# Graph kernel: source one-hots of graph attention made during propagation, and fewer blocks at its last two stages

## What is computed

```python
# L0: ten steps of propagation, w = 1/sqrt(deg(src)*deg(dst)), sums over dst into src
for _ in range(10): out = segment_sum(out[col] * w, row) * 0.9 + h * 0.1
# L1: graph attention (one self loop per node added)
h = x @ W
e = leaky_relu((h @ att_src)[src] + (h @ att_dst)[dst], 0.2)
e = exp(e - segment_max(e, dst)[dst])
out = tanh(segment_sum(h[src] * e[:, None], dst) / segment_sum(e, dst) + bias)
# L2: dot attention, four heads, softmax over the edges of each source
q, k, v = x[rows] @ qW, x[cols] @ kW, x[cols] @ vW ; res = segment_sum(softmax(q.k) * v, rows)
# L3: mean aggregation
out = segment_sum(x[src] @ W + b, dst) / deg
```

## Time and profile before

| | us |
|---|---|
| median of three runs | 1568.0 (1566.27 to 1568.41) |
| the profiled execution | 1561.1 |
| its span, first to last instruction | 1559.3 |
| building counts and buckets | 0 to about 300 |
| propagation, ten turns | about 300 to 838 |
| graph attention: norm, masks and maxima | 840 to 974 |
| graph attention: slot loop | 974 to 1183 |
| dot attention: norm, projection | 1183 to 1223 |
| dot attention: slot loop | 1223 to 1459 |
| mean aggregation | 1464 to 1559 |

### The profile page before, as it was taken

The page is one execution under the profiler, slowest core; times in us unless marked ns, Lnnn a source line. Parts: engine busy times, 40 slices in busy tenths (PEclk is TensorE's granted clock), DMA queues, the critical chain, the costliest instruction groups (busy, mean ns, idle before and its releaser), DMA issues. The chain is left out here.

```text
span 1559.3 us, 45179 instructions
## 1 busy us (share of the span) xinstructions
PE 1244.0 (80%) x18543; PEld 1185.1 (76%) x18544; DVE 1234.2 (79%) x2306; ACT 583.3 (37%) x1271; POOL 355.8 (23%) x211
## 2 busy tenths in 40 slices
PE   4689888399999899998996400888883999999378
PEld 3278777399899899998995300888883899999378
DVE  6989888577677677676756899999996899999733
ACT  0057788200000000000000686566664677777311
POOL 1400000000000000000001010688882455555200
PEclk7868888699999999999998655999996999999689
DMA  0013334386678577676621474555534276775382
GB/s 11 0 61 115 121 114 141 104 334 266 225 272 287 208 277 275 219 262 251 245 73 54 154 261 161 213 213 213 213 130 193 89 270 263 279 283 221 141 332 90
DMA packets 88813, 297.54 MB, mean 191 GB/s; under 512 B 22399, under 2 KB 23976, under 8 KB 88604
## 3 DMA queue, kind: packets, MB, share of 16 engines
q1 hardware_dynamic: 66668, 231.86, 41.2%
q10 hardware_dynamic: 21600, 61.45, 10.3%
q0 software_dynamic: 336, 1.20, 0.3%
HBM read 188.31 MB, written 106.16 MB: 189 GB/s over the span
## 5 line engine op out<-in xcount | busy, mean ns | idle before, releaser
L1327 PE MATMUL psum<-work,count 128*128 128x192 f16 x6250 | 523.7, 248 | 35.7 <-issue 35.7
L1327 PEld LDWEIGHTS psum<-work,count 128*128 128x128 f16 x6250 | 521.6, 99 | 37.8 <-issue 36.9
L964 ACT ACTIVATE work<-work 128x1248 f32<-128x1248 f32 (+1 forms) x6 | 7.2, 1203 | 584.2 <-DVE work L947 584.1
L1672 PE MATMUL psum<-count 128*128 128x98 f16 x625 | 113.2, 209 | 114.6 <-DVE count L1726 99.2
L1718 POOL TENSOR_TENSOR count<-count 128x970 bf16<-128x970 f32 (+1 forms) x75 | 175.5, 2366 | 73.5 <-ACT count L1711 73.5
L1944 PE MATMUL psum<-count 128*128 128x100 f16 (+1 forms) x1875 | 176.6, 207 | 9.8 <-DVE count L2028 7.1
L1246 DVE SCALAR_TENSOR_TENSOR work<-psum,small,work 128x96 f32<-128x96 f32 x250 | 79.3, 317 | 123.7 <-PE psum L1327 123.4
L1945 PE MATMUL psum<-count 128*128 128x100 f16 (+1 forms) x1875 | 176.5, 207 | 0.1
L1944 PEld LDWEIGHTS psum<-count 128*128 128x128 f16 x1875 | 162.6, 98 | 14.8 <-DVE count L2028 11.1
L1945 PEld LDWEIGHTS psum<-count 128*128 128x128 f16 x1875 | 164.1, 98 | 0.2 <-issue 0.2
L2007 POOL TENSOR_TENSOR count<-count 128x1000 bf16<-128x1000 f32 (+1 forms) x75 | 133.1, 1775 | 108.2 <-ACT count L1993 108.2
(11 more groups left out here) (290 smaller groups left out, 2733.7 us busy)
## 6 DMA issues: line engine op xcount, KB each, us to landing
count<-onehots_by_src SPq DMA_DIRECT2D x75, 800.0 KB, 6.7
count<-bucket_rows_by_dst SPq DMA_DIRECT2D x50, 800.0 KB, 4.3
x<-bucket_rows_by_src SPq DMA_DIRECT2D x75, 400.0 KB, 5.8
onehots_by_src<-x ACTq DMA_DIRECT2D x75, 400.0 KB, 6.1
count_f<-count SPq DMA_DIRECT2D x25, 800.0 KB, 7.5
count<-count_turned SPq DMA_DIRECT2D x25, 800.0 KB, 5.6
count<-count_f SPq DMA_DIRECT2D x17, 800.0 KB, 4.2
count_turned<-x SPq DMA_DIRECT2D x25, 416.0 KB, 2.4
```

The lines of the kernel that those rows point to most:

```text
L1327: last = nc.tensor.matmul(bank[i % BANKS], count16[:, j, i * P:(i + 1) * P], y[par][:, j, :], start=(j == 0), stop=(j == TILES - 1))
L1672: nc.tensor.matmul(ps[:, at:at + GW], node_hot[SRC][t % 2][:, s, :], high[:, s, :], start=True, stop=False, skip_group_check=True)
```

## The change

What it does:

1. In propagation 50 more node halves are made and stored: graph attention's source one-hots, 128 x 1600 each, to a new tensor in HBM. There are now 150 node halves and 50 edge halves, three to one, placed behind the updates of tiles 0 to 22 of the first nine turns, 200 in 207 slots. Each is one load of 400 KB, one compare and one store of 400 KB. A tile of the counts is stored behind every sixth load.
2. In graph attention's slot loop the compare of the source nodes is gone (25 of 128 x 3200). SyncE loads the finished one-hots instead of the spread rows, 800 KB a tile as before, into four buffers instead of two; its wait is now for the tile's gathering by TensorE.
3. The work that makes the next round's one-hots moves from its own block into the main blocks of both slot loops, behind their last instructions and behind a branch.
4. Mean aggregation's second block is merged into its layer norm block; semaphores take the barrier's place. SyncE loads twelve tiles ahead without a stop.

The diff's core (the rest is the passing of arguments and the same thing for several rounds):

```diff
@@ propagate
-    pieces = Pieces(node_halves, steps_space.take(HALF_TILES[0][1] * P, F16), ...)
+    pieces = Pieces(node_halves, 0, 6 * TILES, steps_space.take(HALF_TILES[0][1] * P, F16), ...)
     LAST = K_STEPS - 1
-    assert LAST * 20 >= PIECES * 6 // 5
+    TURNS = 23
+    SLOTS = LAST * TURNS
...
-                        q = 20 * turn + i - 1
-                        if turn < LAST and 1 <= i <= 20 and q % 6 < 5:
-                            spots.compare(dve, pieces, 5 * (q // 6) + q % 6)
+                        q = TURNS * turn + i
+                        if turn < LAST and i < TURNS and (q + 1) * pieces.total // SLOTS > q * pieces.total // SLOTS:
+                            spots.compare(dve, pieces, q * pieces.total // SLOTS)
@@ Spots.row, Spots.one_hot: node halves from 4 * TILES on
+        return self.by_dst[bass.ds(k, 1), w - 2 * TILES, SRC].rearrange("k s n -> k (s n)")[:, half * HALF_ROW:(half + 1) * HALF_ROW]
+        hots = self.hot_by_src[:, w, :] if w < 2 * TILES else self.hot_by_dst[:, w - 2 * TILES, :]
@@ graph_attention
+    source_hot = [node_hot[SRC][0], *(v.rearrange("p (t n) -> p t n", n=P) for v in spread[SRC]), node_hot[SRC][1]]
+    SOURCES = len(source_hot)
...
+    def load_source_hot(sp, t):
+        sp.dma_start(source_hot[t % SOURCES].rearrange("p t n -> p (t n)"), hot_by_dst[:, t, :]).then_inc(S["source_hot_%d" % (t % SOURCES)], 16)
...
+                for t in range(2, SOURCES):
+                    load_source_hot(sp, t)
                 for t in range(2, TILES):
-                    for i, v in enumerate((SRC, DST)):
-                        sp.wait_ge(S["node_hot"], 2 * (t - 2) + i + 1)
-                        load_spread(sp, k, t, v)
+                    sp.wait_ge(S["node_hot"], t - 1)
+                    load_spread(sp, k, t)
+                    if t + 2 < TILES:
+                        sp.wait_ge(S["gathered"], (t - 1) * PER)
+                        load_source_hot(sp, t + 2)
...
                         if s0 == 0:
-                            pe.wait_ge(S["node_hot"], 2 * t + 2)
+                            pe.wait_ge(S["source_hot_%d" % (t % SOURCES)], 16 * (t // SOURCES + 1))
+                            pe.wait_ge(S["node_hot"], t + 1)
...
-                spot_nodes(SRC, 0)
-                spot_nodes(DST, 0)
+                spot_nodes(0)
                 spot_edges(0)
...
                             if s0 == 0:
-                                spot_nodes(SRC, t + 1)
+                                spot_nodes(t + 1)
                             elif s0 == GROUP:
-                                spot_nodes(DST, t + 1)
-                            else:
                                 spot_edges(t + 1)
@@ both slot loops, VectorE (SyncE and ScalarE alike)
                 add(TILES - 2)
-                add(TILES - 1)
+                def add_and_compare():
+                    add(TILES - 1)
+                    following.compare(dve)
+                if_one(dve, m, lambda: add(TILES - 1), add_and_compare)
-        spot_next_round(nc, m, pieces, k + 1, ids_dram, by_src, hot_by_src)
@@ mean_aggregate
-        if_one(sp, m, lambda: load_first(sp, 0, 2 * UNDER_WAY))
-        sp.wait_ge(weights_loaded, 32)
+        if_one(sp, m, lambda: one_loads(sp), lambda: count_loads(sp))
+        store(sp)
...
+                if s == 0:
+                    pe.wait_ge(parts_set, 2)
                 for j in range(TILES):
+                    for k, (t0, _) in enumerate(HALVES_OF_NODES):
+                        if s == 0 and j == t0:
+                            pe.wait_ge(low_made, k + 1)
...
     def one_loads(sp):
-        load_first(sp, 2 * UNDER_WAY, READY)
+        load_first(sp, 0, READY)
...
-    with nc.Block() as block:
-        @block.sync
+    layernorm_relu(nc, m["norm"], x, h, sq, ..., ready, sync=load_ahead, tensor=products, gpsimd=set_up, vector_before=dot_vector_end,
+                   vector_between=identity_and_inverse, vector_after=low_parts, scalar_after=scalar_end)
```

More of the change, by code:

```diff
@@ L968, in _, with __init__, load, compare @@
             scalar_after(act)
-def spot_next_round(nc, m, pieces, k, ids_dram, by_src, hot_by_src):
-    spots = m["spots"]
-    with nc.Block() as block:
-        @block.sync
[L976 to L996, removed]
+class NextRound:
+    def __init__(self, m, pieces, k, ids_dram):
+        self.m, self.pieces, self.k, self.ids_dram = m, pieces, k, ids_dram
+    def load(self, sp):
+        if self.pieces.edge is not None:
+            self.m["spots"].load_ids(sp, self.pieces, self.k, self.ids_dram)
+        for n in range(self.pieces.nodes):
+            self.m["spots"].load(sp, self.pieces, self.k, n)
+        self.m["spots"].wait_stored(sp, self.pieces)
+    def compare(self, dve):
+        dve.sem_inc(self.m["spots"].counted, 1)
+        for piece in range(self.pieces.total):
+            self.m["spots"].compare(dve, self.pieces, piece)
+        self.m["spots"].wait_stored(dve, self.pieces)
+    def store(self, act):
+        self.m["spots"].stores(act, self.pieces)
+        self.m["spots"].wait_stored(act, self.pieces)
 class Residual:
@@ L1140, in propagate, with is_edge, edge_of, node_of @@
+    def is_edge(self, piece):
+        return self.per > 0 and piece % self.per == 1
+    def edge_of(self, piece):
+        return piece // self.per
+    def node_of(self, piece):
+        if not self.per:
+            return piece
+        group, i = divmod(piece, self.per)
+        return group * (self.per - 1) + i - (i > 1)
+def propagate(nc, m, ins, cnt_dram, cnt16_dram, ids_dram, by_src, by_dst):
     W = TILES * D
@@ L1277, in _ @@
             spots.load_ids(sp, pieces, 0, ids_dram)
-            for n in range(NODE_HALVES):
-                spots.load(sp, pieces, 0, n, by_src)
+            for n in range(pieces.nodes):
+                spots.load(sp, pieces, 0, n)
                 store_count_tile(n)
@@ L1296, in _ @@
         def _(act):
-            spots.stores(act, pieces, hot_by_src)
+            spots.stores(act, pieces)
         @block.tensor
@@ L1360, in propagate, with _ @@
     with nc.Block() as block:
+        @block.gpsimd
+        def _(pool):
+            clear_semaphores(nc, spots.all())
         @block.vector
@@ L1652, in graph_attention @@
     with nc.Fori(0, rounds_of(nc, m)) as k:
+        following = NextRound(m, pieces, k + 1, ids_dram)
         with nc.Block() as block:
```

212 lines of the change are left out of this document (118 added, 94 removed).

## The result

| | before | after |
|---|---|---|
| median | 1567.1 us (1563.0 to 1568.4, 4 runs) | 1606.6 us (1604.8 to 1612.2, 4 runs) |
| ratio | | 1.0265 (95%: 1.0237 to 1.0293) |
| profiled execution, its span | 1561.1, 1559.3 | 1612.2, 1610.4 |

The changed kernel is 2.7% slower. The forecast was 1551, and 1606.6 lies above the whole range. I divide the 51.1 us first, stage by stage.

What follows compares the result with a forecast made beforehand. It took graph attention's slot loop as bound by what VectorE's compares and GpSimd share, and propagation by TensorE. Terms -17.5 + 10 - 4 - 6 = -17.5 us, from a median of 1568.0 to 1551 us, range 1534 to 1578.

Steps and rivals of the forecast that it cites:

- Parts 3 and 4: Next round's work moved behind dot attention, -4 us; mean aggregation in one block, first matmul earlier, -6 us.
- Part 1: Graph attention's slot loop without source compares: 7.91 us a tile falls to 7.2, -17.5 us, bounds -8 and -28.
- the turns: Graph attention's loop: VectorE's compares and GpSimd's subtractions exclude each other; each removed compare brings 0.85 us, 0.70 taken.
- rival (c): Graph attention's loop hardly gains, VectorE's time becoming waits for ScalarE or GpSimd: 7.8 us a tile, -3, 1565; chance 0.12.
- The floor: Graph attention's loop: the lower bound is TensorE's 6.8 us a tile, a gain of -28 us; as a rival, chance 0.15.
- Part 2: Propagation with 50 more compares, loads and stores: +10 us, bounds 0 and +40.
- the buffers' cycle: Propagation: load, compare, store and gaps take 12.6 us for four halves; 52.5 us a turn against 51.
- The bandwidth reckoning: Propagation: demand of 388 GB/s inside the 23 slots lies within the 318 to 413 seen in 2 us stretches.
- (a): Propagation becomes bound by its transfers, buffers' cycle longer than 13.5 us: +40 instead of +10, 1580 us; chance 0.16.

Runs made afterwards that it cites:

- e1_ends_only: The kernel before with only the next round's work moved into dot attention's slot loop and mean aggregation in one block: 1556.4 us, ratio 0.9937.
- g1_edges_third: The changed kernel with the old propagation, the edge compare of graph attention's loop in the third group of slots instead of the second: 1536.6 us, ratio 0.9812.
- three buffers: The kernel before with three buffers for node halves in place of four, no other work changed: 1573.0 us.
- counts late: The changed kernel with the count tiles' stores moved behind the last load, into propagation's tenth turn: 1592.9 us.
- all 25 slots: The changed kernel with its 200 pieces spread over all 25 tiles of a turn instead of tiles 0 to 22: 1601.8 us.
- five buffers: The changed kernel with a fifth node buffer in propagation, room made by leaving some one-hots and ids out: 1562.7 us.
- five, counts late: The changed kernel with a fifth node buffer and the count tiles stored in propagation's tenth turn: 1572.5 us.

## Why the prediction was wrong, step by step

**Parts 3 and 4 were right.** -4 and -6 were forecast; the rows give -4.0 and, to the first matmul, -6.1, of which 1.2 us is given back inside the stage. `e1_ends_only` gives 9.9 us for both.

**Part 1 was right on the turns and failed on the list of what moves.** The two engines do take turns, a removed compare is worth far less than its 2.04 us of busy time (19.0 us over 25 tiles are 0.76), and `g1_edges_third` shows the tile of 7.2 us and a loop 19.0 us shorter than before (208.0 - 189.0), where -17.5 was forecast. But the prediction never priced that the edge compare goes to the second group. There it begins during GpSimd's second subtraction, as at 1110.79, and ends 1.68 us behind it, with the weighing, the rounding and the next subtraction after it. That is the step that failed in the loop: -17.5 us was forecast and -0.4 came. So rival (c) came true in its size, for another reason than the one given: VectorE's time didn't move into the wait for ScalarE, it is one compare that stands in GpSimd's way. "Against it: VectorE has no idle time now" was no argument, since idle time appeared at once, 9 us in 50, and changed nothing. The floor was also taken wrongly: not TensorE's 6.8 us a tile but the ring of GpSimd and ScalarE, 7.35 us in the tile shown, which the third group's place already reaches (189.0 us for the loop against 189.5). So that the 7.2 us of the forecast were met in `g1_edges_third` is in part luck: the sum had taken one turn of 0.85 us from three, but there the edge compare's turn is off the chain too, and the ring stops the gain at the same figure.

The Trainium skill, SBUF — State Buffer, section "SBUF: two separate sides", which has the two engines exclude each other for whole instructions, is borne out by these rows: the same edge compare takes 1.81 us begun just as a subtraction ends, and 2.87 us begun 1.19 us before one's end (1110.79 against 1111.98). The rule should have been applied to the moved compare too.

**Part 2 failed in one step of the buffers' cycle.** Its sum was right: 12.6 us for load, compare and store; with the changed kernel's own landings, 6.2 and 5.8, it is 6.2 + 0.63 + 5.8 + 0.5 = 13.1. What failed is what it was held against. The prediction compared with a whole turn of 51 us, 1.5 us too little, and let pauses cover part of that. But the halves lie in 23 slots of a turn, and the loads can only run ahead by the number of buffers. Between two uses of one buffer lie, in the changed kernel, 4 x 207/150 = 5.5 slots of 2.04 us, **11.3 us**. That is 1.8 us too little for every group of four, and not 1.5 us for a whole turn. With each kernel's own numbers (needed: its median landings and 1.13 us; given: its buffers, slots and halves):

| kernel | needed | given | short by | propagation |
|---|---|---|---|---|
| before | 12.6 | 4 x 180/100 slots = 14.7 | none | 540.6 (546 in the middle of its kind) |
| three buffers | 11.3 | 3 x 180/100 = 11.0 | 0.3 | 551.0 |
| changed | 13.1 | 4 x 207/150 = 11.3 | 1.8 | 600.9 |
| counts late | 12.5 | 11.3 | 1.2 | 576.0 |
| all 25 slots | 14.0 | 4 x 225/150 = 12.2 | 1.8 | 589.5 |
| five buffers | 14.3 | 5 x 207/150 = 14.1 | 0.2 | 554.7 |
| five, counts late | 13.3 | 14.1 | none | 553.2 |

The landings in the second column are each kernel's own, measured afterwards, and they scatter: over the five profiles with the old propagation the loads' median lay between 5.7 and 6.2 us. With the 12.6 us of before, which the prediction had, the changed kernel would be short by 1.3 us, and 1.3 x 150/4 groups is 49 us.

The shortage orders the kernels: with 0.3 us or none propagation takes 541 to 555 us, with 1.2 us 576, with 1.8 us 590 and 601. For the changed kernel 1.8 us x 150/4 groups is 67 us against some 55 measured over its kind; turn ends give some back. The size is not derived more closely than that, and differences of 10 us between rows are within the scatter; a landing is no constant: the medians of the runs went from 4.9 to 6.8 us.

The second thing missed is what a stall costs beyond its length. A turn's end in the changed kernel (VectorE, TensorE, and TensorE's stretches after it):

```profile
527.45 0.64 DVE L1093 TENSOR_SCALAR x<-x,small 128x1600 f16<-128x1600 f16 x1 [4.12 <-DMA x<-bucket_rows_by_src]
...
542.65 0.64 DVE L1093 TENSOR_SCALAR x<-x,small 128x1600 f16<-128x1600 f16 x1 [1.58 <-DMA x<-bucket_rows_by_src]
...
544.77 7.41 PE L1345 MATMUL psum<-work,count 128*128 128x192 f16 x60 [5.02 <-DVE work L1270]
...
548.99 0.32 DVE L1264 SCALAR_TENSOR_TENSOR work<-psum,small,work 128x96 f32<-128x96 f32 x1 [3.46 <-PE psum L1345]
...
545.00:548.00 3.00, 3.00 (x21) 2.85 (x20) 0.47 (x2) 0.00 (x0) 0.00 (x0) 0.50 0.92 369
548.00:551.00 3.00, 3.00 (x29) 2.92 (x28) 1.66 (x5) 0.00 (x0) 0.00 (x0) 0.74 0.60 178
551.00:554.00 3.00, 3.00 (x40) 3.00 (x37) 2.47 (x7) 0.00 (x0) 0.00 (x0) 1.00 0.70 276
```

A load is 4.12 us late at 527.45 and another 1.58 us at 542.65; TensorE, which at a turn's end can't run ahead, stands idle for 5.02 us up to 544.77. Then the granted clock is 0.50, the 1.2 GHz level, and 21 matmuls pass in 3 us, then 29, then 40. Against 40 each time some 30 matmuls are missing, another 2.4 us at the pace of the earlier trace rows, 20 us for 245. And VectorE, having caught up, waits 3.46 us for the next tile. Over propagation that shows as TensorE's busy time for the same matmuls. The changed kernel:

```profile
299.00:899.00 600.00, 541.56 (x6232) 532.47 (x6233) 392.39 (x1193) 0.00 (x0) 0.18 (x1) 0.94 0.79 280
```

and the kernel before:

```profile
300.00:840.00 540.00, 522.39 (x6236) 520.54 (x6237) 370.22 (x1144) 0.00 (x0) 0.18 (x1) 0.98 0.65 235
```

So the 60.3 us are 50.8 of waiting for VectorE, 19.2 of slower matmuls, and 10.0 less at the loop's later starts, 60.0 together. (Of the pauses before "issue", 25.0 us now and 35.7 in the earlier trace rows, the longest, 17.9 and 18.6 us, lies before the first matmul and so outside; 7.1 and 17.1 are left.) Whether those pauses hid in the new waits isn't shown.

**The bandwidth reckoning pointed the wrong way.** 388 GB/s of demand inside the slots was held against what 2 us stretches had shown, and the range of that part, 0 to +40, was made from it. The bytes never were the limit: the changed kernel moves 297 to 305 GB/s in the stretches of its waits, and with a fifth buffer 337 GB/s with TensorE at its full pace. (One word of the reckoning was wrong and its sum right: three pieces before went with half a count tile, not a third, and 2.46 MB is with the half.) In mean aggregation, where tiles of counts are loaded and little is stored, the changed kernel moved more, and for long:

```profile
1530.00:1570.00 40.00, 29.41 (x309) 29.04 (x310) 19.79 (x44) 9.15 (x17) 0.00 (x0) 0.80 1.01 401
```

The Trainium skill's bound of some 358 GB/s between HBM and SBUF (DMA: Bandwidth & Descriptors, section "Where 436 GB/s comes from") was passed there for 40 us, and the measurement decides. In propagation's slots no stretch of 100 us went above 332, so that rule, which was weighed against the change, is not what made it slower.

**The rivals.** (a) named the right place and mechanism, a cycle over what the turns give, though its condition, a cycle above 13.5 us, was not met (13.1), and it named "a single edge buffer, landings of up to 10.3 us" for it, of which the edge buffer had no part (0.5 us of waits). Its chance of 0.16 was too low and its price, +40, fell short of 50. "Against it: today's waits never reached TensorE" was weak, since today's cycle has 2.1 us to spare. And (a) was priced with the loop's whole gain; (a) and (c) came true together: 1568 - 10 + 50 = 1608, against 1606.6. They had been treated as exclusive, each with its own 0.1 to 0.2. Together at the prediction's own prices they would have been 1568 - 3 - 10 + 40 = 1595, above its range of up to 1578 and still 12 us short.

## What to carry to other kernels

Hold a ring of buffers against the time between two uses of one buffer where its work is densest, not against the average of a longer loop, and take the landing time at the load that the change itself brings. Where two engines exclude each other, list every instruction whose place in the order changes, not only those that disappear: one moved compare ate a gain of 18 to 19 us. And before a stage at full pace is filled to the brim, price the stall too: the engine behind restarts slowly.

## What the runs showed of the hardware

- After an idle time of 5.02 us TensorE came back at a granted clock of 0.50 and was at 1.00 again 6 us later; over propagation the same matmuls cost 19 us more.
- The landing time of a 400 KB load isn't fixed: its median was 6.2 us in the changed kernel, 6.8 with pieces in all 25 slots, and 5.3 in the kernel before with three buffers (5.8 with four, and 5.7 to 6.2 over the five profiles with the old propagation). A ring with fewer buffers can thus lose less than a fixed landing would say: with three, 11.3 us were needed and not 12.6.
- A load to 16 of 128 partitions landed in 2.1 us in the median, where the full ones of the same kernel took 6.7; the small ones came later, when the DMA engines were also less busy (share 0.37 from 700 to 800 us, 0.83 from 400 to 500).
- The same comparison on VectorE took 1.81 or 2.87 us, only by where GpSimd's subtraction stood when it began.
- Transfers between HBM and SBUF moved 401 GB/s over 40 us of mean aggregation in the changed kernel (1530 to 1570 us), at a share of 1.01.
